# Cross attention of a fused decoder kernel: block transposes on VectorE and DMAs in place of TensorE's transposes of x

## The chip, the cores and the metric

The kernel runs on one core of one Trainium2 chip. The metric is the device time of one execution in microseconds (us). The time before is the median of three runs.

The engines are written as the profile writes them: PE is TensorE (PEld its weight loads), DVE is VectorE, ACT is ScalarE, POOL is GpSimd and SP is SyncE. SP computes nothing here; it issues DMAs, one instruction after another.

## What is computed

Two decoder layers, each with a self-mixing block, a cross attention and a feed-forward block, every block followed by a sum with its input and a layer norm. The change touches the cross attention of the first layer and the linear block behind it. `x` is 4 x 1024 x 512 (32 tiles of 128 tokens by 512), the context `ctx` has 64 rows for each of the 4 batches, and there are 16 heads of 32:

```python
q = x @ Wq.T + bq                       # for every token
s = (q_h . k_h) / sqrt(32), masked      # 16 heads x 64 keys for every token
p = softmax(s)
x = layernorm(x + (p_h . v_h joined) @ Wo.T + bo)
x = layernorm(x + tanh(x @ W12 + bias)) # the linear block, its weights folded into one matrix
```

All of it is float32. TensorE contracts over the partitions, so for `x @ W` it needs x with features on the partitions, whereas x lies in SBUF with tokens on them. x has to be turned twice in this stage: before the queries, and after the first layer norm before the linear block.

## The kernel before

The stage is `cross_attention_and_linears`. x stays in SBUF as 32 tiles; `x_tile(n)` is one. Each engine runs a list of steps written out by hand, in **slots** `s`: in slot s a tile n = s gets its scores, while tile s-2 is at its output projection, tile s-3 at its linear and so on. The order of an engine's steps inside a slot is the order of the `if there(...)` lines; nothing is scheduled by a compiler. Steps of different engines meet by semaphores, and an engine whose next instruction waits does nothing else.

TensorE's slot s, in order: `transpose_x(s+8)` turns a tile of x by four 128x128 transposes into PSUM (L954), from which ScalarE copies it to `XT` (L1052); `transpose_p(s-2)` turns the softmax weights (L994); `query(s+4)` computes a quarter of the features of the queries of a whole **group** of four tiles (L977), so four slots make one group's queries and the first of them needs all four turned tiles; `weigh(s-2)` (L1002); `transpose_x2(s-3)`, four more transposes (L954, too) for the linear; `scores(s)` (L986); `project(s-2)` (L1012); `linear(s-3)` (L1022).

VectorE's slot s: `biased(s-4)` (L1131), `total(s-1)` (L1102, L1105), `added(s-4)` (L1136 and the statistics L1109, L1111, L1114), `masked(s)` (L1090), the second layer norm's `normal` (L1119), `shifted(s)` (the maximum L1096 and its subtraction L1098, which wait for GpSimd's `hide`, L921), `attended(s-2)` (L1125 and statistics), and the first layer norm's `normal` (L1119 again, which waits for a power that GpSimd takes, L948).

SP issues six loads at the start of the stage and then nothing; `XT` has two halves, `XT[g % 2]` for group g. TensorE's PSUM banks 5 and 6 go round between query, project and linear.

Some moves of the same kind as the new ones exist elsewhere in this kernel: in the last stage VectorE transposes x in 32x32 blocks into `X4B` (L2282) and SP moves the 16 blocks to their places by 16 DMAs (L2025, `tl_XT<-tl_X4B`); in the local attention SP stores block-transposed tiles to DRAM by four DMAs each (L1286, `unit_gT<-tiles`).

## Time and profile before

| what | value |
|---|---|
| median of 3 runs | 2664.42 us (2663.8 to 2665.64) |
| the profiled execution, its own time | 2665.74 us |
| its span in the trace | 2664.0 us |
| the stage in the span | from 394.6 us to 906.1 us |
| TensorE busy over the span | 95% |
| VectorE busy over the span | 73% |

The profiled execution was 1.3 us above the median. The stage's start is TensorE's first transpose at 394.61 us and its end the last layer norm on VectorE (905.50 us and 0.55 us). The page's chain that ended last begins at 1559 us, in the last stage, so it says nothing on this one; the stage has to be read from the timeline of its engines.

### The profile page before, as it was taken

The page shows a single profiled execution, that of the slowest core. Times are in us where ns is not written, and L with a number is a line of the kernel's source. Part 1 is how long each engine was busy: PE and PEld are TensorE (multiplying, and loading weights), DVE is VectorE, ACT ScalarE, POOL GpSimd, SP SyncE. Part 2 cuts the span into 40 slices and gives each one's busy share as a digit, 9 for nine tenths or more (in the row PEclk, how much of TensorE's full clock was granted, in tenths as well). Part 3 has the DMA queues.
Part 4 walks back from the last instruction along what each step waited for, and adds up shares of the span by engine and source line. Part 5 has one row for each costly group of instructions (what it writes and reads, how often), then busy time and mean ns, then how long its engine had stood idle before and what let it go on. Part 6 is the DMA issues. An engine that isn't in the chain of part 4 may idle for free. (4 is left out here: it accounts for less than half of the span.)

```text
span 2664.0 us, 37090 instructions
## 1 busy us (share of the span) xinstructions
PE 2535.6 (95%) x12933; PEld 1562.9 (59%) x12933; DVE 1933.4 (73%) x3292; ACT 732.0 (27%) x1073; POOL 867.0 (33%) x900
## 2 busy tenths in 40 slices
PE   8999998999999898999998869999999999999998
PEld 4444544555555444445444447777777777777775
DVE  4788403666667446777778858888888888888886
ACT  1111222333332125666668711000000000000000
POOL 2322203455555336767677721111111111111000
PEclk9999999999999999999999989999999999999999
DMA  5444121000000043343434441222222222222111
GB/s 177 146 143 178 56 91 42 1 0 1 1 1 1 23 103 96 101 106 97 104 102 129 134 122 42 53 53 53 53 54 54 54 54 54 54 54 54 46 38 38
DMA packets 338726, 183.85 MB, mean 69 GB/s; under 512 B 174031, under 2 KB 304463, under 8 KB 337518
## 3 DMA queue, kind: packets, MB, share of 16 engines
q1 hardware_dynamic: 307862, 156.49, 21.4%
q10 hardware_dynamic: 30680, 24.98, 3.3%
q8 instruction: 106, 1.74, 0.3%
q14 instruction: 78, 0.64, 0.1%
HBM read 90.51 MB, written 52.43 MB: 54 GB/s over the span
## 5 line engine op out<-in xcount | busy, mean ns | idle before, releaser
L2114 PE MATMUL bank<-tiles,tl_XQT 128*128 128x512 f32 (+1 forms) x768 | 323.9, 565 | 1.2 <-issue 1.2
L2119 PE MATMUL bank<-tiles,tl_XQT 128*128 128x512 f32 (+1 forms) x768 | 317.9, 557 | 0.0
L2131 PE MATMUL bank<-tiles,tl_HT 128*128 128x512 f32 x682 | 302.1, 599 | 5.8 <-DMA tl_HT<-tl_tmp 5.8
L2114 PEld LDWEIGHTS bank<-tiles,tl_XQT 128*128 128x128 f32 x768 | 235.6, 309 | 79.8 <-issue 16.0
L2119 PEld LDWEIGHTS bank<-tiles,tl_XQT 128*128 128x128 f32 x768 | 236.7, 308 | 65.6
L2193 ACT ACTIVATE tl_HQ<-bank 128x512 f32<-128x512 f32 (+1 forms) x96 | 54.0, 562 | 803.1 <-PE bank L2114 757.0
L2131 PEld LDWEIGHTS bank<-tiles,tl_HT 128*128 128x128 f32 x682 | 219.3, 324 | 74.4 <-issue 9.4
L1403 POOL TENSOR_SCALAR_AFFINE_SELECT tiles<-tiles 128x512 f32<-128x512 f32 x256 | 184.0, 721 | 169.2 <-ACT tiles L1630 153.8
L2061 POOL TENSOR_TENSOR tl_rs<-tl_ve,mhalf 128x1 f32<-128x1 f32 x29 | 16.0, 551 | 527.5 <-DVE tl_ve L2272 527.5
L1730 DVE SCALAR_TENSOR_TENSOR tiles<-tiles,bank 128x1024 f32<-128x1024 f32 (+1 forms) x128 | 141.7, 1148 | 18.8 <-PE bank L1506 18.7
L1408 POOL TENSOR_SCALAR_AFFINE_SELECT tiles<-tiles 128x512 f32<-128x512 f32 x224 | 152.9, 682 | 0.0
L2053 POOL TENSOR_TENSOR tl_rs<-tl_ve,mhalf 128x1 f32<-128x1 f32 x32 | 18.8, 587 | 393.9 <-DVE tl_ve L2254 393.9
L1630 ACT ACTIVATE tiles<-bank 128x1024 f32<-128x1024 f32 (+1 forms) x128 | 123.5, 965 | 28.1 <-PE bank L1465 28.0
L1635 ACT ACTIVATE tiles<-tiles 128x1024 f32<-128x1024 f32 (+1 forms) x128 | 124.9, 1000 | 20.2 <-DVE tiles L1730 17.2
L1555 PE MATMUL bank<-home_T,tiles 128*128 128x512 f32 x256 | 121.2, 618 | 3.6 <-ACT tiles L1664 0.9
L977 PE MATMUL bank<-space_T 128*128 128x512 f32 x256 | 118.4, 606 | 2.5 <-DVE X L1125 2.3
L1567 PE MATMUL bank<-home_odd,tiles 128*128 128x512 f32 x256 | 117.4, 601 | 0.0
L1022 PE MATMUL bank<-space_T,space_quant 128*128 128x512 f32 x256 | 115.2, 592 | 1.5 <-ACT space_quant L1079 1.5
L1012 PE MATMUL bank<-space_even,space_quant 128*128 128x512 f32 x256 | 115.3, 593 | 1.0 <-ACT space_quant L1074 0.9
L1428 POOL TENSOR_TENSOR la_rn<-la_n,mhalf 128x16 f32<-128x16 f32 x32 | 92.8, 2899 | 52.0 <-DVE la_n L1805 52.0
L2069 PE MATMUL bank<-home_T,attended_values 128*128 128x512 f32 x232 | 106.6, 603 | 0.0
L921 POOL TENSOR_TENSOR xl_SM<-xl_SM,xl_nm 128x1024 f32<-128x1024 f32 x32 | 80.0, 2500 | 78.4 <-DVE xl_SM L1090 78.4
(302 smaller groups left out, 4669.3 us busy)
## 6 DMA issues: line engine op xcount, KB each, us to landing
tl_HT<-tl_tmp SPq DMA_DIRECT2D x248, 44.0 KB, 2.0
tl_HT<-tl_tmp ACTq DMA_DIRECT2D x248, 44.0 KB, 2.0
fp_weights<-space_quant ACTq DMA_DIRECT2D x33, 256.0 KB, 2.1
X<-in_x SPq DMA_DIRECT2D x8, 1024.0 KB, 10.2
v<-tiles SPq DMA_DIRECT2D x32, 256.0 KB, 2.4
unit_g<-tiles SPq DMA_DIRECT2D x32, 256.0 KB, 2.5
unit_gT<-tiles SPq DMA_DIRECT2D x128, 64.0 KB, 2.1
la_GN<-unit_g SPq DMA_DIRECT2D x128, 64.0 KB, 2.1
```

Source lines behind the costliest of these rows:

```text
L977: mm = e.matmul(bank[turn(s, 0)][:, :], WqT[:, c, m * P:(m + 1) * P], XT[g % 2][:, c, :], start=(c == 0), stop=(c == C - 1))
L1012: mm = e.matmul(bank[turn(s, 1)][:, :], AT[:, c, :], WoT[:, c, :], start=(c == 0), stop=(c == C - 1))
L1403: return e.affine_select(out=x[:, :, 0:P], in_=x[:, :, 0:P], compare_op=ALU.is_ge, fill=fill, base=0, pattern=[[0, HC], [1, P]], channel_m ...
L1408: return e.affine_select(out=x[:, :, P:WIN], in_=x[:, :, P:WIN], compare_op=ALU.is_ge, fill=fill, base=0, pattern=[[0, HC], [-1, P]], chan ...
L1555: mm = e.matmul(bank[1][:, :], XT[m % 2][:, c, :], WgT[:, c, :], start=(c == 0), stop=(c == C - 1))
L1567: mm = e.matmul(bank[2][:, :], XT[m % 2][:, c, :], WvT[:, c, :], start=(c == 0), stop=(c == C - 1))
L1630: e.activation(TR[p % RING][:, :, 0:cols(t)], four(ARG[:, :])[:, :, 0:cols(t)], ACT.Tanh).then_inc(s_T.sem, 1)
L1635: e.activation(y, y, ACT.Exp).then_inc(s_p.sem, 1)
L1730: e.scalar_tensor_tensor(out=y, in0=y, scalar=1.0, in1=d, op0=ALU.add, op1=ALU.mult).then_inc(s_u.sem, 1)
L2114: mm = e.matmul(bank[(2 * q) % 3][:, 0:w], chunk(XQT[n % 2], c), WgT[q][:, :, c, :], start=(c == 0), stop=(c == C - 1))
L2119: mm = e.matmul(bank[(2 * q + 1) % 3][:, 0:w], chunk(XQT[n % 2], c), WuT[q][:, :, c, :], start=(c == 0), stop=(c == C - 1))
L2131: mm = e.matmul(bank[DOWN][:, :], chunk(HT, q), WdT[:, q, :], start=(q == 0), stop=(q == IC - 1))
```

## The change

The first eight tiles are still turned by TensorE. For tiles 8 to 31, VectorE transposes the tile in 32x32 blocks into `XB` (`x_turned`) and SP moves the blocks to `XT` by 16 DMAs (`x_moved`), each of 32 partitions x 4 x 32 elements. For the linears of tiles 0 to 29, VectorE transposes the tile into `XB2` (`x2_turned`), SP stores it to a DRAM buffer by 4 DMAs of 32 x 4 x 128 elements (`x2_stored`), and ScalarE issues one load of it into `XL`; tiles 30 and 31 still go by TensorE. The linear moves from the end of slot n+3 to slot n+4, right behind the query. On VectorE `added` and its layer norm move one slot later too, and `biased` moves behind `added`. The stage has one slot more. The weights' layout of the linear is unchanged; `XL` is read with a stride of four elements.

```diff
...
+        self.X2d = self.dram("x2_turned", (2, P, D))
...
+        XB = [sb(f"XB{n}", [P, D]) for n in range(2)]
+        s_xt, d_xt = sem("x_turned"), [sem(f"xT_moved{n}") for n in range(2)]
...
+        BY_PE = 2 * B
         x_bank = lambda n: n if n < B else XTB
+        later = lambda n: BY_PE <= n < NT
...
-        SLOTS = range(-2 * B, NT + 5)
+        SLOTS = range(-2 * B, NT + 6)
+
+
+        by_blocks = lambda n: 0 <= n < NT - 2
+        XB2 = [sb(f"XB2{n}", [P, D]) for n in range(2)]
+        XLT = XL[:, :, :].rearrange("p c t -> p (c t)")
+        in_chunks = lambda x: x.rearrange("p (t c) -> p c t", c=C)
+        s_tu, d_tu, d_xl = sem("x2_turned"), [sem(f"x2_stored{n}") for n in range(2)], sem("x2T_load")
...
+                def x_moved(n):
+                    g, at = n // B, n % B * P
+                    e.wait_ge(s_xt.sem, s_xt.at(n - BY_PE + 1))
+                    e.wait_ge(s_q.sem, s_q.at(C * (g - 1)))
+                    for i in range(4):
+                        for j in range(4):
+                            e.dma_start(XT[g % 2][32 * j:32 * j + 32, :, at + 32 * i:at + 32 * i + 32],
+                                        XB[n % 2][32 * i:32 * i + 32, :].rearrange("p (c j t) -> p j c t", c=C, j=4)[:, j]
+                                        ).then_inc(d_xt[n % 2].sem, 16)
+
+                def x2_stored(n):
+
+                    e.wait_ge(s_tu.sem, s_tu.at(n + 1))
+                    e.wait_ge(d_xl.sem, d_xl.at(16 * (n - 1)))
+                    for i in range(4):
+                        e.dma_start(k.X2d[n % 2].rearrange("(j p) w -> p j w", j=4)[:, :, P * i:P * i + P],
+                                    XB2[n % 2][32 * i:32 * i + 32, :].rearrange("p (j w) -> p j w", j=4)).then_inc(d_tu[n % 2].sem, 16)
...
+                for s in SLOTS:
+                    if by_blocks(s - 3):
+                        x2_stored(s - 3)
+                    if later(s + 2 * B):
+                        x_moved(s + 2 * B)
...
                 def transpose_x2(n):
                     e.wait_ge(s_x2.sem, s_x2.at(n + 1))
-                    e.wait_ge(s_tc.sem, s_tc.at(min(n + 12, NT)))
-                    e.wait_ge(s_xe.sem, s_xe.at(n))
+                    e.wait_ge(s_tc.sem, s_tc.at(BY_PE))
+                    e.wait_ge(s_xe.sem, s_xe.at(n - NT + 2))
                     transposed(XTB, x_tile(n), s_xl)
...
                 def query(i):
 
                     g, m = i // C, i % C
-                    e.wait_ge(s_tc.sem, s_tc.at(B * g + B))
+                    e.wait_ge(s_tc.sem, s_tc.at(min(B * g + B, BY_PE)))
+                    for d in d_xt:
+                        e.wait_ge(d.sem, d.at(256 * (B // 2) * (g - 1)))
                     s = i - B
                     e.wait_ge(s_qe.sem, s_qe.at(i - 1))
-                    e.wait_ge(s_a2.sem, s_a2.at(s - 2))
+
+                    e.wait_ge(s_lbd.sem, s_lbd.at(s - 4))
...
+                    e.wait_ge(s_qe.sem, s_qe.at(min(s + B + 1, NT)))
+                    e.wait_ge(s_lbd.sem, s_lbd.at(n - 2))
+                    for c in range(C):
+                        mm = e.matmul(bank[turn(s, 2)][:, :], AT[:, c, :], WoT[:, c, :], start=(c == 0), stop=(c == C - 1))
+                    mm.then_inc(s_o.sem, 1)
+
+                def linear(n):
+                    s = n + 4
+                    if by_blocks(n):
+                        e.wait_ge(d_xl.sem, d_xl.at(16 * (n + 1)))
+                    else:
+                        e.wait_ge(s_xe.sem, s_xe.at(n - NT + 3))
+
+                    e.wait_ge(s_a2.sem, s_a2.at(min(s - 2, NT)))
                     e.wait_ge(s_lbd.sem, s_lbd.at(n - 1))
                     for c in range(C):
-                        mm = e.matmul(bank[turn(s, 1)][:, :], AT[:, c, :], WoT[:, c, :], start=(c == 0), stop=(c == C - 1))
-                    mm.then_inc(s_o.sem, 1)
-
-                def linear(n):
-                    s = n + 3
-                    e.wait_ge(s_xe.sem, s_xe.at(n + 1))
-
-                    e.wait_ge(s_qe.sem, s_qe.at(min(s + B + 1, NT)))
-                    e.wait_ge(s_a2.sem, s_a2.at(min(n, NT)))
-                    for c in range(C):
-                        mm = e.matmul(bank[turn(s, 2)][:, :], XL[:, c, :], WF[:, c, :], start=(c == 0), stop=(c == C - 1))
+                        mm = e.matmul(bank[turn(s, 1)][:, :], in_chunks(XLT)[:, c, :], WF[:, c, :], start=(c == 0), stop=(c == C - 1))
                     mm.then_inc(s_l.sem, 1)
...
-                    if there(s + 2 * B):
+                    if 0 <= s + 2 * B < BY_PE:
                         transpose_x(s + 2 * B)
                     if there(s - 2):
                         transpose_p(s - 2)
                     if there(s + B):
                         query(s + B)
+                    if there(s - 4):
+                        linear(s - 4)
                     if there(s - 2):
                         weigh(s - 2)
-                    if there(s - 3):
+                    if there(s - 3) and not by_blocks(s - 3):
                         transpose_x2(s - 3)
                     if there(s):
                         scores(s)
                     if there(s - 2):
                         project(s - 2)
-                    if there(s - 3):
-                        linear(s - 3)
...
-                    if there(s - 3):
+                    if by_blocks(s - 3):
                         n = s - 3
-                        e.wait_ge(s_xl.sem, s_xl.at(n + 1))
+                        e.wait_ge(d_tu[n % 2].sem, d_tu[n % 2].at(64 * (n // 2 + 1)))
                         e.wait_ge(s_l.sem, s_l.at(n))
-                        e.activation(XL[:, :, :], four(bank[XTB][:, :]), ACT.Copy).then_inc(s_xe.sem, 1)
+                        e.dma_start(XLT, k.X2d[n % 2]).then_inc(d_xl.sem, 16)
+                    elif there(s - 3):
+                        n = s - 3
+                        e.wait_ge(s_xl.sem, s_xl.at(n - NT + 3))
+                        e.wait_ge(s_l.sem, s_l.at(n))
+                        e.activation(in_chunks(XLT), four(bank[XTB][:, :]), ACT.Copy).then_inc(s_xe.sem, 1)
+                    if there(s - 4):
+                        n = s - 4
+                        e.wait_ge(s_lbd.sem, s_lbd.at(n + 1))
+                        e.activation(TH[:, :], TH[:, :], ACT.Tanh).then_inc(s_th.sem, 1)
...
+                def x_turned(n):
+                    e.wait_ge(d_xt[n % 2].sem, d_xt[n % 2].at(256 * ((n - BY_PE) // 2)))
+                    e.transpose(XB[n % 2][:, :], x_tile(n)).then_inc(s_xt.sem, 1)
+
+                def x2_turned(n):
+                    e.wait_ge(s_x2.sem, s_x2.at(n + 1))
+                    e.wait_ge(d_tu[n % 2].sem, d_tu[n % 2].at(64 * (n // 2)))
+                    e.transpose(XB2[n % 2][:, :].rearrange("p (j r c) -> p c j r", j=4, r=32), x_tile(n)).then_inc(s_tu.sem, 1)
...
                 for s in SLOTS:
+                    if there(s - 1):
+                        total(s - 1)
+                    if there(s - 5):
+                        added(s - 5)
                     if there(s - 4):
                         biased(s - 4)
-                    if there(s - 1):
-                        total(s - 1)
-                    if there(s - 4):
-                        added(s - 4)
                     if there(s):
                         masked(s)
-                    if there(s - 4):
-                        normal(s - 4, mv3, rs3, s_r3, s_x3)
+                    if there(s - 5):
+                        normal(s - 5, mv3, rs3, s_r3, s_x3)
+                    if later(s + 2 * B + 1):
+                        x_turned(s + 2 * B + 1)
                     if there(s):
                         shifted(s)
                     if there(s - 2):
                         attended(s - 2)
                         normal(s - 2, mv2, rs2, s_r2, s_x2)
+                    if by_blocks(s - 2):
+                        x2_turned(s - 2)
...```

On PE, one early slot of the kernel before (slot 6). `ident` with `X` is a transpose of x, `xl_SM` are the softmax weights, `space_T` alone is a query:

```order
L954 MATMUL bank<-ident,X 128x128 x4
L994 MATMUL bank<-ident,xl_SM 128x128 x8
L977 MATMUL bank<-space_T 128x512 x4
L1002 MATMUL bank<-xl_PT,space_quant 64x128 x8
L954 MATMUL bank<-ident,X 128x128 x4
L986 MATMUL bank<-space_quant,space_T 128x256 x4
L1012 MATMUL bank<-space_even,space_quant 128x512 x4
L1022 MATMUL bank<-space_T,space_quant 128x512 x4
```

And the same slot of the changed kernel (L1018 is the query, L1067 the linear, L1054 the projection):

```order
L1035 MATMUL bank<-ident,xl_SM 128x128 x8
L1018 MATMUL bank<-space_T 128x512 x4
L1067 MATMUL bank<-space_T,space_quant 128x512 x4
L1043 MATMUL bank<-xl_PT,space_quant 64x128 x8
L1027 MATMUL bank<-space_quant,space_T 128x256 x4
L1054 MATMUL bank<-space_even,space_quant 128x512 x4
```

Both groups of transposes of X are gone, the linear stands ahead of `weigh` and the scores, and the query waits for the DMAs of both halves of `XB` (the loop over `d_xt` in the diff).

On SP, the stage's first slots of the changed kernel; the kernel before has no row here. `space_T` is `XT`, and `x_turned` is the DRAM buffer of the linears.

```order
L938 DMA home_bias<-in_L_attn_bg 128x512
L921 DMA space_T<-xl_XB 32x4x32 x48
L930 DMA x_turned<-xl_XB 32x4x128 x4
L921 DMA space_T<-xl_XB 32x4x32 x16
L930 DMA x_turned<-xl_XB 32x4x128 x4
L921 DMA space_T<-xl_XB 32x4x32 x16
```

These are the moves of tiles 8, 9 and 10 (48 DMAs), the store of tile 0, the move of tile 11, the store of tile 1 and the move of tile 12. From there on each slot has one store for the linears and then one move for the queries, in this order.

On DVE, of one slot of the changed kernel, from `masked` on:

```order
L1139 TENSOR_TENSOR xl_SM<-bank,xl_mf 128x1024
L1168 TENSOR_SCALAR X<-X,xl_mv,xl_rs 128x512
L1190 STREAM_TRANSPOSE xl_XB<-X 128x512
L1145 TENSOR_REDUCE xl_mx<-xl_SM 128x16
L1147 TENSOR_TENSOR xl_SM<-xl_SM,xl_mx 128x1024
L1174 TENSOR_TENSOR X<-bank,X 128x512
L1158 BN_STATS xl_st<-X 128x6
L1160 BN_AGGR xl_mv<-xl_st 128x2
L1163 TENSOR_SCALAR xl_ve<-xl_mv 128x1
L1168 TENSOR_SCALAR X<-X,xl_mv,xl_rs 128x512
L1195 STREAM_TRANSPOSE xl_XB<-X 128x4x128
L1151 TENSOR_REDUCE xl_sm<-xl_SM 128x16
```

The kernel before has the same rows without the two STREAM_TRANSPOSE, and with the bias of the linear ahead of the last row here.

## Rows read from the trace of the kernel before

**Rows 1.** Page: engine totals (busy us, share, instructions).
```profile
span 2664.0 us, 37090 instructions
PE 2535.6 (95%) x12933; PEld 1562.9 (59%) x12933; DVE 1933.4 (73%) x3292; ACT 732.0 (27%) x1073; POOL 867.0 (33%) x900
```

**Rows 2.** Timeline, PE, one slot: start, us, engine, line, operation, count.
```profile
717.59 0.60 PE L954 MATMUL bank<-ident,X 128*128 128x128 f32 x4
718.02 1.04 PE L994 MATMUL bank<-ident,xl_SM 128*128 128x128 f32 x8
718.90 3.60 PE L977 MATMUL bank<-space_T 128*128 128x512 f32 x8
722.42 1.09 PE L1002 MATMUL bank<-xl_PT,space_quant 128*64 128x128 f32 x16
723.45 0.66 PE L954 MATMUL bank<-ident,X 128*128 128x128 f32 x4
723.94 1.89 PE L986 MATMUL bank<-space_quant,space_T 128*128 128x256 f32 x8
725.67 3.60 PE L1012 MATMUL bank<-space_even,space_quant 128*128 128x512 f32 x8
729.11 3.60 PE L1022 MATMUL bank<-space_T,space_quant 128*128 128x512 f32 x8
```

**Rows 3.** Timeline, DVE, slot 22; in brackets the idle before and its releaser.
```profile
740.83 1.23 DVE L1090 TENSOR_TENSOR xl_SM<-bank,xl_mf 128x1024 f32<-128x1024 f32 x1 [1.92 <-PE bank L986]
741.97 0.54 DVE L1119 TENSOR_SCALAR X<-X,xl_mv,xl_rs 128x512 f32<-128x512 f32 x1
744.74 1.22 DVE L1096 TENSOR_REDUCE xl_mx<-xl_SM 128x16 f32<-128x1024 f32 x1 [2.23 <-POOL xl_SM L921]
749.62 0.55 DVE L1119 TENSOR_SCALAR X<-X,xl_mv,xl_rs 128x512 f32<-128x512 f32 x1 [0.67 <-POOL xl_rs L948]
...
755.78 1.22 DVE L1090 TENSOR_TENSOR xl_SM<-bank,xl_mf 128x1024 f32<-128x1024 f32 x1 [1.92 <-PE bank L986]
```

**Rows 4.** Timeline, DVE: `masked` of slots 24, 28, 29 and 31.
```profile
770.29 1.23 DVE L1090 TENSOR_TENSOR xl_SM<-bank,xl_mf 128x1024 f32<-128x1024 f32 x1 [1.48 <-PE bank L986]
...
826.83 1.22 DVE L1090 TENSOR_TENSOR xl_SM<-bank,xl_mf 128x1024 f32<-128x1024 f32 x1
839.89 1.23 DVE L1090 TENSOR_TENSOR xl_SM<-bank,xl_mf 128x1024 f32<-128x1024 f32 x1
...
866.55 1.23 DVE L1090 TENSOR_TENSOR xl_SM<-bank,xl_mf 128x1024 f32<-128x1024 f32 x1 [0.48 <-PE bank L986]
```

**Rows 5.** One line's instructions, DVE: count, ns min/median/max, first and last start.
```profile
L2282 DVE STREAM_TRANSPOSE tl_X4B<-X x30: 703/705/711, 1569.0 to 2515.1; 128x512 f32<-128x512 f32 x30
L2400 DVE STREAM_TRANSPOSE tl_QB<-tl_XQ x31: 1082/1116/1144, 1594.9 to 2602.8; 128x512 f32<-128x512 f32 x31
```

**Rows 6.** Timeline, SP: a store by 4 DMAs, a move by 16; then landing.
```profile
1010.85 1.95 SPq L1286 DMA_DIRECT2D unit_gT<-tiles  x4
2014.39 10.33 SPq L2025 DMA_DIRECT2D tl_XT<-tl_X4B  x16
L2025 SPq DMA_DIRECT2D tl_XT<-tl_X4B x480: 591/601/1442, 1569.7 to 2525.5; - x160
DMA to landing us min/median/max: 1.8/1.8/3.0
```

**Rows 7.** Timeline, DVE: the first layer norm of tile 0.
```profile
449.64 0.55 DVE L1119 TENSOR_SCALAR X<-X,xl_mv,xl_rs 128x512 f32<-128x512 f32 x1 [0.69 <-POOL xl_rs L948]
```

**Rows 8.** Timeline, PE, after waits; the first is `query(7)`, the others as cut there.
```profile
447.96 5.37 PE L977 MATMUL bank<-space_T 128*128 128x512 f32 x8 [2.27 <-DVE X L1125]
...
464.69 0.59 PE L977 MATMUL bank<-space_T 128*128 128x512 f32 x1
...
763.32 1.88 PE L977 MATMUL bank<-space_T 128*128 128x512 f32 x4
```

**Rows 9.** Windows: PE, PEld, DVE, ACT, POOL busy, then PEclk, DMA share, GB/s.
```profile
446.00:448.00 2.00, 0.04 (x1) 0.07 (x1) 1.97 (x3) 0.75 (x1) 0.00 (x0) 1.00 0.00 0
448.00:451.50 3.50, 3.50 (x5) 1.44 (x6) 2.71 (x6) 1.71 (x3) 0.57 (x1) 0.62 0.01 2
860.00:864.00 4.00, 2.52 (x21) 2.19 (x22) 3.23 (x7) 2.42 (x4) 0.55 (x1) 0.73 0.00 0
```

**Rows 10.** Timeline, PE and DVE: the start of the next stage, the end of this.
```profile
905.50 0.55 DVE L1119 TENSOR_SCALAR X<-X,xl_mv,xl_rs 128x512 f32<-128x512 f32 x1 [0.67 <-POOL xl_rs L939]
908.97 5.69 PE L1555 MATMUL bank<-home_T,tiles 128*128 128x512 f32 x8 [0.94 <-ACT tiles L1664]
```

More of the change, by code:

```diff
@@ L930, in add_bias @@
                         e.wait_ge(s_lb.sem, s_lb.at(32))
-                    e.wait_ge(s_t.sem, s_t.at(n + 1))
+                    e.wait_ge(s_t.sem, s_t.at(min(n + 1, BY_PE)))
+                    e.wait_ge(s_xt.sem, s_xt.at(n - BY_PE + 1))
                     e.tensor_tensor(x_tile(n), x_tile(n), bo[:, :], ALU.add).then_inc(s_xb.sem, 1)
@@ L936, in _ @@
                         weights(s - 1)
-                    if there(s - 4):
-                        e.wait_ge(s_v3.sem, s_v3.at(s - 3))
+                    if there(s - 5):
+                        e.wait_ge(s_v3.sem, s_v3.at(s - 4))
                         e.tensor_tensor(rs3[:, :], ve3[:, :], k.mhalf[:, 0:1], ALU.pow).then_inc(s_r3.sem, 1)
@@ L957, in transpose_x @@
                 def transpose_x(n):
-                    e.wait_ge(s_xe.sem, s_xe.at(n - 11))
                     if n > B:
@@ L1047, in _ @@
                 for s in SLOTS:
-                    if there(s + 2 * B):
+                    if 0 <= s + 2 * B < BY_PE:
                         n = s + 2 * B
                         e.wait_ge(s_t.sem, s_t.at(n + 1))
-                        e.wait_ge(s_q.sem, s_q.at(C * (n // B - 1)))
-                        e.activation(XT[(n // B) % 2][:, :, (n % B) * P:(n % B + 1) * P], four(bank[x_bank(n)][:, :]), ACT.Copy).then_inc(s_tc.sem, 1)
+                        e.activation(XT[n // B][:, :, (n % B) * P:(n % B + 1) * P], four(bank[x_bank(n)][:, :]), ACT.Copy).then_inc(s_tc.sem, 1)
                     if there(s - 2):
@@ L1057, in _ @@
                         e.activation(PT[:, :, :], PTB.rearrange("p (n t) -> p n t", n=H // 2), ACT.Copy).then_inc(s_pe.sem, 1)
-                    if there(s - 4):
-                        n = s - 4
-                        e.wait_ge(s_lbd.sem, s_lbd.at(n + 1))
-                        e.activation(TH[:, :], TH[:, :], ACT.Tanh).then_inc(s_th.sem, 1)
                     if there(s + B):
@@ L1124, in attended @@
                     e.wait_ge(s_xb.sem, s_xb.at(n + 1))
-                    e.tensor_tensor(y, bank[turn(n + 2, 1)][:, :], y, ALU.add).then_inc(s_a2.sem, 1)
+                    e.tensor_tensor(y, bank[turn(n + 2, 2)][:, :], y, ALU.add).then_inc(s_a2.sem, 1)
                     statistics(n, y, st2, mv2, ve2, s_a2, s_t2, s_m2, s_v2, s_r2)
@@ L1130, in biased @@
                     e.wait_ge(s_a3.sem, s_a3.at(n))
-                    e.tensor_tensor(TH[:, :], bank[turn(n + 3, 2)][:, :], lb[:, :], ALU.add).then_inc(s_lbd.sem, 1)
+                    e.tensor_tensor(TH[:, :], bank[turn(n + 4, 1)][:, :], lb[:, :], ALU.add).then_inc(s_lbd.sem, 1)
                 def added(n):
@@ L1142, in _ @@
                 for s in SLOTS:
+                    if there(s - 1):
+                        total(s - 1)
+                    if there(s - 5):
+                        added(s - 5)
                     if there(s - 4):
                         biased(s - 4)
-                    if there(s - 1):
-                        total(s - 1)
-                    if there(s - 4):
-                        added(s - 4)
                     if there(s):
                         masked(s)
-                    if there(s - 4):
-                        normal(s - 4, mv3, rs3, s_r3, s_x3)
+                    if there(s - 5):
+                        normal(s - 5, mv3, rs3, s_r3, s_x3)
+                    if later(s + 2 * B + 1):
+                        x_turned(s + 2 * B + 1)
                     if there(s):
```

## The prediction, made before the changed kernel ran

> **What bounds the kernel now.** I read the page's totals first: TensorE is busy 95% of the span [rows 1]. The page's chain lies in the last stage, which is not touched, so I went to TensorE's timeline inside this stage. A slot there begins 14.95 us after the last one and has no idle time between its groups; the two groups of four transposes take 718.02 - 717.59 = 0.43 us and 723.94 - 723.45 = 0.49 us of it, the query 3.52, `weigh` 1.03, the scores 1.73, projection and linear 3.44 each and the transpose of the weights 0.88 [rows 2]. VectorE is next: from one `masked` to the end of its slot it works or waits for its own chain for 13.0 us, and then idles 1.92 us for TensorE's scores [rows 3]. In slots 28 and 29, where TensorE has no query left, `masked` no longer waits and the spacing is 839.89 - 826.83 = 13.06 us [rows 4]. That is VectorE's own round. SP is idle in the stage.
>
> **TensorE's part.** From slot 0 the slot loses 0.43 and 0.49 us and becomes 14.02 us. If nothing else came, 24 tiles for queries and 30 for linears would give 24 x 0.43 + 30 x 0.49 = 25 us. ScalarE loses the two copies behind them and has room.
>
> **VectorE's part.** `x_turned` has the form of L2282: 0.71 us. It stands behind the first `normal` (which ends at 742.51), where VectorE waits until 744.74 for GpSimd [rows 3], so it costs nothing; without that wait it would cost 0.7 us a slot. `x2_turned` writes with a stride of four as L2400 does: 1.12 us rather than 0.71 [rows 5]; I take 1.12, since the output's stride is the same. It stands behind the second `normal`, with no wait ahead of it that it could fill. VectorE's round becomes 13.06 + 1.12 = 14.18 us, just above TensorE's 14.02. So VectorE sets the slot, and by this alone it gains 14.95 - 14.18 = 0.77 us.
>
> **SP's part, on which I rest the forecast.** In every slot SP issues 4 DMAs for the linears, then 16 for the queries. The nearest rows, of the same shapes, give 1.95 us for four stores and 10.33 us for sixteen moves, 0.646 us apart, and 1.8 us until one lands [rows 6]. 12.3 us fits into a slot. But look at when it starts. The query that opens group g (slot 4g-4) needs tile 4g+3. Its move stands on SP in slot 4g-5 behind the store of tile 4g-8, and this store waits for `x2_turned(4g-8)`, which is VectorE's work of slot 4g-6, done only when TensorE is already in slot 4g-5. The loop from one such query to the next, four slots on, is then a chain:
> - query 3.52, linear 3.44, `weigh` 1.03, scores until their end 1.89: 9.9 us, with `masked` behind it [rows 2];
> - from `masked` to the end of the second `normal`, 749.62 + 0.55 - 740.83 = 9.34 us [rows 3], and `x2_turned` 1.12: 10.5 us. This turns tile 4g-6, seen from the query of group g;
> - two rounds of VectorE to `x2_turned(4g-4)`: 28.4 us;
> - on SP, the store 1.95, fifteen spacings 9.69, the last landing 1.8: 13.4 us, and the query of group g+1 may start.
>
> The sum is 62.2 us. Four slots without a wait would be 56.7 us by VectorE and 56.1 by TensorE; TensorE thus stands still for about 6 us before each group's first query. Before, four slots take 59.8 us. The change takes away a cost of 0.9 us a slot and puts a wait of 6 us in every fourth one.
>
> **The clock behind the wait.** After an idle time of 2.27 us the query at 447.96 takes 5.37 us instead of 3.60, 1.8 us more [rows 8], and the granted clock there is 0.62, in part the lower level of 1.2 GHz, after 1.00 [rows 9]. After over 5 us idle, the first matmuls of the next stage need 5.69 us for what takes 3.60 at full clock, 2.1 us more [rows 10]. I take 2.1 us for each wait; it falls into the first link of the chain (query, linear), so it counts in full. The ends are 0 (the clock is kept) and 2.7 (half clock for 5.4 us). The loop becomes 62.2 + 2.1 = 64.3 us, 4.5 more than before.
>
> **The sum**, against the profiled execution's 2665.74 us:
> - Up to query(8): the layer norm of tile 0 ends at 450.19 us [rows 7]; 1.12 + 13.4 us of transposition and SP bring the query to 464.8 us; before it is at 464.69 [rows 8]. 0 us. The wait is there too, in place of the transposes.
> - From query(8) to query(28), five loops: 5 x 4.5 = +22.5 us.
> - Query(28) to its slot's `masked`: before 770.29 - 763.32 = 7.0 us [rows 4, 8]; now 9.9, since the linear stands between, and 2.1 of clock: +5.0 us.
> - `masked` of slot 24 to slot 31: before 866.55 - 770.29 = 96.3 us [rows 4]; now 7 x 14.18 = 99.3: +3.0 us. The transposes that are gone no longer help here, the one on VectorE still costs.
> - In slots 28 to 31 TensorE idles some 3.7 us of each slot, and the clock falls as it does at 860 us, 0.73 [rows 9], where two slots took 866.55 - 839.89 = 26.7 us instead of 26.1 [rows 4]: +1 us, ends 0 and 7 (half clock on the whole path from scores on in four slots).
> - From there to the end of the stage, 906.05 - 866.55 = 39.5 us [rows 4, 10], the linears of tiles 30 and 31 wait for nothing new: 0 us, at most +2.
>
> Together +31.5 us: 2697.2 us for the profiled execution, and, 1.3 us lower as before, 2696 us for the median. So the change makes it 1.2% slower; a measurement of this kernel tells about 0.2% (5 us) from no change.
>
> **A rule of the Trainium skill.** Sixteen DMAs in a row held SP for 10.33 us while one took 1.8 us to land [rows 6], so here the issue is the long part. The Trainium skill says in "DMA: Bandwidth & Descriptors", section "Issuing engines are not separate DMA queues", that the sequencer's time to start a DMA is usually small relative to the DMA itself. By that rule rival 1 would hold; the trace speaks against it. The page "VectorE: DVE Perf Modes", section "Rules for kernel authors", advises TensorE for a transpose of 128x128 where PSUM will do, which speaks against this change without a price.
>
> **Rivals.**
> 1. *The moves come in time, and it gets faster.* If SP needs so little that the last landing is no later than the unstalled query, 6 us sooner (13.4 down to 7.4 us, 0.27 us per move), VectorE's round alone sets 20 slots: query(8) to query(28) takes 283.6 us instead of 298.6, and the query's way to `masked` +2.9, the tail +3.0. With some 4 us of wait left out at the start that is -13 us: 2651 us. It turns at a gain of 4.5 us a loop, a spacing near 0.35 us with the clock's cost, 0.50 without. The smallest of 480 such issues was 0.591 us [rows 6], so 10%.
> 2. *The clock is kept*: no 2.1 us in six waits, none in the tail: 2696 - 13.6 = 2682 us. Against it stand [rows 8 to 10]; 10%.
> 3. *The landing takes longer*: 3.0 us is the longest seen [rows 6], and the tail's clock costs its 7 us: 6 x 1.2 + 6 = +13, 2709 us. Sixteen moves, a store and ScalarE's load share the DMA engines in each slot, as comparable ones do in the last stage. 12%.
> 4. *The change does nothing*: the loop takes as long as before, 59.8 us, because part of the wait goes and the clock stays: 2659 to 2670 us; 5%.
> 5. My forecast's own case, 58%; 5% is left for something slower still, above 2716 us.
>
> **How the numbers follow.** 2696 us is the likeliest case. Its own unknowns: spacing 0.59 to 0.65 (-0.8 us a wait), the clock's cost 0 to 2.7 us, the landing, the tail. Taking in rivals 2 and 3 the range is 2674 to 2716 us and leaves out rivals 1 and 4 and the far end, two in ten. Faster by over 0.2%: 0.11 (rival 1 and a little of 4), within 0.2%: 0.05, slower: 0.84.
>
> **What the profile after would show.** On TensorE's timeline, waits of 5 to 7 us before queries 8, 12, 16, 20, 24 and 28, released by the DMA `space_T<-xl_XB`, and a granted clock near 0.5 right behind them; the other three slots of a group near 14.1 us. On SP, 16 moves in 10.3 us, starting when 4 stores of 1.95 us are done, and these starting at `x2_turned`. On VectorE, transposes of 0.71 and 1.12 us, and a spacing of 14.2 us between the `masked` of the last slots. I am wrong if the spacing of the moves is far below 0.6 us, if the query's wait is missing, or if another wait, such as ScalarE's load of `XL` before the linear (it should have some 5 us to spare), comes in its place.

## The result, and the profile after

| what | before | changed |
|---|---|---|
| median of four runs each | 2665.03 us (2663.8 to 2668.03) | 2702.34 us (2698.55 to 2702.8) |
| ratio, 95% interval | | 1.0137 (1.0125 to 1.015) |
| profiled execution, own time | 2665.74 us | 2702.51 us |
| its span | 2664.0 us | 2700.8 us |
| end of the stage in the span | 906.05 us | 942.29 us |

The change makes the kernel 37 us slower, 1.4%. The stage ends 36.2 us later and the rest of the program takes 0.6 us more, so the loss is in the stage. A note for all comparisons below: in the profiled executions of all kernels the unchanged code behind the stage took 1755.0 to 1760.8 us, so differences of a few us are read from the stage's own length and not from the medians.

The page of the changed kernel, its totals and the groups of query and linear (busy us, mean ns | idle us before them):

```profile
PE 2532.9 (94%) x12717; PEld 1577.7 (58%) x12717; DVE 1978.5 (73%) x3346; ACT 698.5 (26%) x1019; POOL 865.3 (32%) x900
L1018 PE MATMUL bank<-space_T 128*128 128x512 f32 x256 | 130.5, 659 | 37.0 <-issue 37.0
L1067 PE MATMUL bank<-space_T,space_quant 128*128 128x512 f32 x256 | 120.1, 614 | 16.5 <-issue 15.3
```

Against [rows 1] TensorE has 216 matmuls fewer and is busy only 2.7 us less. The query's line says why: its 32 queries take 130.5 us, 4.08 us each, though a query at full clock takes 3.60, and TensorE sat idle for 37.0 us ahead of them. TensorE's timeline shows where; this is one slot without and one with the wait (start, duration, in brackets the idle time before it):

```profile
504.04 3.60 PE L1054 MATMUL bank<-space_even,space_quant 128*128 128x512 f32 x8
507.47 1.04 PE L1035 MATMUL bank<-ident,xl_SM 128*128 128x128 f32 x8
508.35 3.60 PE L1018 MATMUL bank<-space_T 128*128 128x512 f32 x8
...
521.60 1.04 PE L1035 MATMUL bank<-ident,xl_SM 128*128 128x128 f32 x8
528.30 5.83 PE L1018 MATMUL bank<-space_T 128*128 128x512 f32 x8 [5.67 <-issue]
533.97 3.60 PE L1067 MATMUL bank<-space_T,space_quant 128*128 128x512 f32 x8
537.49 1.10 PE L1043 MATMUL bank<-xl_PT,space_quant 128*64 128x128 f32 x16
538.52 1.99 PE L1027 MATMUL bank<-space_quant,space_T 128*128 128x256 f32 x8
```

A slot without the wait now takes 521.60 - 507.47 = 14.13 us, against 14.95 before [rows 2]. The query at 528.30 opens a group; it starts after 5.67 us of nothing and takes 2.2 us longer. The same query of the other groups:

```profile
464.04 5.53 PE L1018 MATMUL bank<-space_T 128*128 128x512 f32 x8 [8.38 <-issue]
...
592.88 5.96 PE L1018 MATMUL bank<-space_T 128*128 128x512 f32 x8 [5.68 <-issue]
657.57 6.05 PE L1018 MATMUL bank<-space_T 128*128 128x512 f32 x8 [5.67 <-issue]
722.37 6.07 PE L1018 MATMUL bank<-space_T 128*128 128x512 f32 x8 [5.70 <-issue]
787.36 6.00 PE L1018 MATMUL bank<-space_T 128*128 128x512 f32 x8 [5.86 <-issue]
```

These are queries 8, 16, 20, 24 and 28. 8.38 + 5.67 + 5.68 + 5.67 + 5.70 + 5.86 is the 37.0 us of the page. "issue" says that the profile has no record that ended the wait; what the query waits for in the code are the sixteen moves of the group's last tile, and their rows on SP end 1.4 us before it (from issue to landing one takes 1.8 us in the median):

```profile
514.76 1.76 SPq L930 DMA_DIRECT2D x_turned<-xl_XB  x4
516.62 10.25 SPq L921 DMA_DIRECT2D space_T<-xl_XB  x16
528.86 1.76 SPq L930 DMA_DIRECT2D x_turned<-xl_XB  x4
530.72 10.26 SPq L921 DMA_DIRECT2D space_T<-xl_XB  x16
551.07 1.76 SPq L930 DMA_DIRECT2D x_turned<-xl_XB  x4
```

516.62 + 10.25 = 526.87 is the end of the last issue of tile 15, the last of the group that query 12, at 528.30, opens. SP does nothing between 541.0 and 551.07: it is not full, it is late, because the store waits for VectorE. VectorE's rows around the wait:

```profile
527.75 1.09 DVE L1195 STREAM_TRANSPOSE xl_XB<-X 128x512 f32<-128x512 f32 x1
...
537.60 0.69 DVE L1180 TENSOR_TENSOR xl_TH<-bank,xl_lb 128x512 f32<-128x512 f32 x1 [5.79 <-PE bank L1067]
540.55 1.23 DVE L1139 TENSOR_TENSOR xl_SM<-bank,xl_mf 128x1024 f32<-128x1024 f32 x1 [2.26 <-PE bank L1027]
...
549.94 1.11 DVE L1195 STREAM_TRANSPOSE xl_XB<-X 128x512 f32<-128x512 f32 x1
```

`x2_turned` ends at 528.84 and 551.05, and SP's stores start at 528.86 and 551.07. VectorE itself stands still for 5.79 and 2.26 us, for TensorE. So this is the loop of the prediction: query, `masked`, `x2_turned`, store, moves, next group's query. Cut at these rows, from 528.30 to the query at 592.88: 12.25 us to `masked` (540.55), 10.50 to the end of `x2_turned` (551.05), 28.25 for two slots (549.94 to 578.19 by `masked` at 540.55 and 568.80), and 13.58 for SP and the landing; 64.58 us.

The granted clock around the wait (window, PE, PEld, DVE, ACT, POOL busy, then PEclk, DMA share, GB/s):

```profile
522.30:528.30 6.00, 0.33 (x4) 0.12 (x2) 5.17 (x8) 1.97 (x2) 1.73 (x2) 0.79 0.16 26
528.30:533.00 4.70, 4.70 (x6) 2.02 (x7) 3.37 (x7) 0.00 (x0) 2.72 (x2) 0.54 0.25 63
533.00:544.00 11.00, 11.00 (x45) 6.83 (x44) 2.99 (x4) 1.80 (x3) 2.08 (x1) 1.00 0.23 46
```

It falls within the idle time, stands near 0.5, the level of 1.2 GHz, for the query, and is back at 1.00, 2.4 GHz, with the linear. In the last slots TensorE has a new wait, ahead of the linear, sometimes with the lower clock behind it and sometimes not:

```profile
849.26 5.49 PE L1067 MATMUL bank<-space_T,space_quant 128*128 128x512 f32 x8 [2.84 <-issue]
...
864.84 3.79 PE L1067 MATMUL bank<-space_T,space_quant 128*128 128x512 f32 x8 [2.83 <-issue]
...
878.83 3.79 PE L1067 MATMUL bank<-space_T,space_quant 128*128 128x512 f32 x8 [2.94 <-issue]
...
906.80 5.49 PE L1067 MATMUL bank<-space_T,space_quant 128*128 128x512 f32 x8 [2.94 <-issue]
```

These are slots 28, 29, 30 and 32. The linear's row of the page, 16.5 us of idle time, is mostly this wait.

### The profile page after: what moved, and what is told of

Read it like the earlier page. It is cut to its first block and busy times, and to the rows that moved or that the text cites. A ratio compares the mean times of both kernels' runs of the same rounds, so it can differ in the third digit from the quotient of the medians.

```text
span 2700.8 us, 37250 instructions
## 1 busy us (share of the span) xinstructions
PE 2532.9 (94%) x12717; PEld 1577.7 (58%) x12717; DVE 1978.5 (73%) x3346; ACT 698.5 (26%) x1019; POOL 865.3 (32%) x900
## 5 line engine op out<-in xcount | busy, mean ns | idle before, releaser
L1018 PE MATMUL bank<-space_T 128*128 128x512 f32 x256 | 130.5, 659 | 37.0 <-issue 37.0
L1067 PE MATMUL bank<-space_T,space_quant 128*128 128x512 f32 x256 | 120.1, 614 | 16.5 <-issue 15.3
L1054 PE MATMUL bank<-space_even,space_quant 128*128 128x512 f32 x256 | 115.3, 593 | 0.8 <-ACT space_quant L1114 0.7
L1067 PEld LDWEIGHTS bank<-space_T,space_quant 128*128 128x128 f32 x256 | 78.6, 310 | 53.4 <-issue 27.1
```

The source lines that it names most:

```text
L1018: mm = e.matmul(bank[turn(s, 0)][:, :], WqT[:, c, m * P:(m + 1) * P], XT[g % 2][:, c, :], start=(c == 0), stop=(c == C - 1))
L1067: mm = e.matmul(bank[turn(s, 1)][:, :], in_chunks(XLT)[:, c, :], WF[:, c, :], start=(c == 0), stop=(c == C - 1))
```

## Experiments

My theory: the loop through SP's queue costs a wait in each group, because (a) each move stands behind a store that waits for VectorE, (b) sixteen issues take 10.3 us, and (c) the wait lowers the clock. Rivals: the wait is the landing's or the DMA engines'; the linears' way through DRAM costs the time; the clock plays no part. Each diff is against the changed kernel. Medians, ratios to the kernel before with their 95% intervals, and the stage from `masked(0)` to its last layer norm's end in the profiled execution. The kernel before was measured again beside them, 2665.79 us beside the first four variants (to "queries alone") and 2666.1 us beside the other four:

| kernel | median us | ratio to before | stage, us |
|---|---|---|---|
| before | 2665.79, 2666.1 | | 486.3 |
| changed | 2702.34 | 1.0137 (1.0125 to 1.015) | 523.0 |
| moves first | 2655.53 | 0.9964 (0.9952 to 0.9977) | 480.4 |
| TensorE kept busy | 2691.75 | 1.01 (1.0086 to 1.0115) | 512.9 |
| half the moves | 2663.72 | 0.9995 (0.9986 to 1.0004) | 484.2 |
| queries alone | 2663.84 | 0.9995 (0.9987 to 1.0004) | 484.3 |
| linears alone | 2666.09 | 0.9999 (0.999 to 1.0008) | 484.9 |
| moves first, busy last slots | 2656.93 | 0.9969 (0.9957 to 0.998) | 478.7 |
| moves first, own banks | 2649.0 | 0.9935 (0.9923 to 0.9948) | 470.2 |
| the same, linears by blocks to tile 24 | 2643.87 | 0.9923 (0.9909 to 0.9936) | 464.7 |

### The moves ahead of the store

```diff
                 for s in SLOTS:
-                    if by_blocks(s - 3):
-                        x2_stored(s - 3)
                     if later(s + 2 * B):
                         x_moved(s + 2 * B)
+                    if by_blocks(s - 3):
+                        x2_stored(s - 3)
```

> Only the order on SP is changed: in each slot the 16 moves of a tile for the queries stand ahead of the 4 stores of a tile for the linears. Theory (the move waits, through the store ahead of it, for VectorE's work on another tile): a move starts as soon as its own tile is turned, some 9 us sooner, the wait before each group's first query (5.7 us) and the half clock behind it go, and each slot takes TensorE's 14.12 us. Query(28) then comes 282.4 us after query(8) instead of 323.3, query(8) itself some 6 us sooner, and of the part behind query(28) 2.9 + 3.6 + 3.1 us over before remain: about 2652 us, 0.5% faster than before. Rival A (there is too much issue time on SP, whatever the order: 12.1 us and the landings): the wait stays at several us, only the victim changes, and the linears wait for XL; 2680 us or more. Rival B (VectorE's two transposes set the slot): no wait at the queries, but slots above 14.2 us and waits for VectorE; 2660 us or more.

SP does the same work in another order, and 2702 us become 2655.5: faster than the kernel before, though not the 2652 us expected (the last slots, below). No query waits but the first of group 2. SP's rows at the place of the wait above (the same view):

```profile
514.76 10.25 SPq L921 DMA_DIRECT2D space_T<-xl_XB  x16
525.11 1.99 SPq L930 DMA_DIRECT2D x_turned<-xl_XB  x4
528.88 11.00 SPq L921 DMA_DIRECT2D space_T<-xl_XB  x16
```

A run of sixteen still takes 10.25 us. It starts every 14.12 us and ends well before its query, so the length of the run alone did not make the wait: its place behind the store did. The slots take 14.12 us throughout. But the last four are long:

```profile
740.00:795.00 55.00, 55.00 (x222) 33.87 (x221) 41.99 (x68) 15.20 (x21) 29.89 (x22) 1.00 0.14 39
795.00:811.00 16.00, 13.16 (x51) 7.59 (x50) 11.65 (x18) 3.72 (x5) 7.39 (x6) 0.89 0.18 50
811.00:826.00 15.00, 12.17 (x48) 6.95 (x47) 10.28 (x18) 3.08 (x4) 7.02 (x5) 0.89 0.11 36
```

Each of slots 28 to 31 has 2.84 us of idle time, then a linear of 5.1 to 5.5 us (these are TensorE's rows), and `masked` comes every 15.4 us on the mean, 61.54 us for four (794.92 to 856.46):

```profile
802.02 5.11 PE L1067 MATMUL bank<-space_T,space_quant 128*128 128x512 f32 x8 [2.84 <-issue]
817.22 5.49 PE L1067 MATMUL bank<-space_T,space_quant 128*128 128x512 f32 x8 [2.83 <-issue]
```

### TensorE kept busy through the wait

Six matmuls that nobody reads stand ahead of the first query of groups 2 to 7.

```diff
                     e.wait_ge(s_tc.sem, s_tc.at(min(B * g + B, BY_PE)))
+                    if g >= 2 and m == 0:
+                        for _ in range(6):
+                            e.matmul(bank[XTB][:, :], WqT[:, 0, 0:P], WF[:, 0, :], start=True, stop=True)
                     for d in d_xt:
```

> The changed kernel with six matmuls (128x512, into an unused bank, result not read) ahead of the first query of each group from the third on, in the place of the wait: 6 x 0.858 = 5.1 us of TensorE's work where it stands idle for 5.7 to 8.4 us. Theory (the clock falls in the wait and costs 2.3 us behind it): the query takes 3.6 us instead of 5.5 to 6.1, the loop of four slots falls from 64.7 to about 62.4 us, and six of these give 12 to 14 us: about 2689 us. Rival (the query is slow because the DMAs write XT and the SBUF is busy, or the clock doesn't matter because the chain goes another way): the loop stays at 64.7 us and the time at 2702 us.

2691.75 us, 10.6 less than the changed kernel, with work added. The query at the same place:

```profile
518.71 5.32 PE L1013 MATMUL bank<-space_T 128*128 128x512 f32 x12
524.43 3.67 PE L1021 MATMUL bank<-space_T 128*128 128x512 f32 x8 [0.41 <-issue]
```

It still comes when the moves have landed, but at full speed. The loop is 62.3 us (524.43 to 586.73) in place of 64.6, so the clock costs 2.3 us a loop; the other 2.5 us over the 59.8 of before are the chain. Six times 2.3 would be 13.8, and 13.9 us are won up to `masked` of slot 24; 4.2 of them are lost again in the last four slots, which are all long here (61.8 us, 826.10 to 887.86, against 57.6, 842.16 to 899.71).

### Half of the moves

Only eight of the sixteen DMAs of each tile are issued, so for tokens 64 to 127 of the later tiles the queries read what was there before.

```diff
-                    for i in range(4):
+                    for i in range(2):
                         for j in range(4):
...
-                        e.wait_ge(d.sem, d.at(256 * (B // 2) * (g - 1)))
+                        e.wait_ge(d.sem, d.at(128 * (B // 2) * (g - 1)))
...
```

> Of the 16 DMAs that move a tile for the queries only 8 are issued (token rows 0 to 63; the other half of XT keeps old values, so the queries of these tokens are wrong). SP's order is that of the changed kernel. Theory (the loop is a chain with SP's issue time in it): SP's link is 8 x 0.646 = 5.2 us shorter, the wait falls from 5.7 to about 0.5 us, the clock is kept, and the loop is TensorE's 4 x 14.12 = 56.5 us plus 0.5: five loops give 38 us, the first wait and clock some 7 more: about 2656 us. Rival A (a landing or the DMA engines' load sets the time, not the issue): the wait falls by less than half. Rival B (VectorE's chain alone): no change, 2702 us.

The order on SP is that of the changed kernel, and the wait shrinks from 5.7 to 0.5 us (TensorE's queries 12 and 16):

```profile
515.80 3.67 PE L1018 MATMUL bank<-space_T 128*128 128x512 f32 x8 [0.52 <-issue]
...
573.06 3.67 PE L1018 MATMUL bank<-space_T 128*128 128x512 f32 x8 [0.53 <-issue]
```

The loop is 57.26 us: the 64.3 us of the prediction less eight spacings of 0.64 and less 2.1 of clock give 57.1. So the count of issues, 0.6 us each, is the other half of the cause; the landing is no shorter here (median 1.9 us against 1.8 in the changed kernel). The time, 2663.7 us, missed the expected 2656. The five loops gave 34.5 us in place of 38 (745.71 - 456.85 = 288.86 us against 323.32). And from `masked` of slot 24 to that of slot 31 this kernel needs 102.65 us (755.80 to 858.45) against 99.93, since here, too, three of the last four slots take 15.2 to 15.6 us. I had not put that into the expectation.

### Each half of the change alone

Without blocks for the linears (`by_blocks` is never true), SP has only the moves:

```diff
-        by_blocks = lambda n: 0 <= n < NT - 2
+        N2 = 0
+        by_blocks = lambda n: 0 <= n < N2
...
```

> Only the queries' x goes by blocks; the linears' x is turned by TensorE and copied by ScalarE for all 32 tiles, at its new place in the order. No x2_turned on VectorE, no stores on SP. Theory: nothing stands ahead of the moves on SP, no wait; TensorE's slot is 14.12 + 0.4 = 14.5 us up to slot 31 where it sets the pace, VectorE's round 13.06; 20 slots x (14.95 - 14.5) = 9 us gained, some 5 lost by the linear that stands between query and scores and by the slot more: about 2660 us, 0.2% faster than before. Rival (the moves alone, 10.3 us on SP with landing, already come late): waits of some us at the groups' first queries, 2675 us or more.

And without blocks for the queries, SP has only the stores:

```diff
-        BY_PE = 2 * B
+        BY_PE = NT
...
-                    for d in d_xt:
-                        e.wait_ge(d.sem, d.at(256 * (B // 2) * (g - 1)))
...
```

> Only the linears' half of the change: x for the queries is turned by TensorE for all 32 tiles, SP has only the four stores of a slot. Theory (the sixteen moves behind the store are what makes the queries wait): no idle time of over 1 us ahead of any query, every slot of TensorE near 14.12 + 0.44 = 14.57 us (VectorE's round 13.99 less 0.71 us of the first transposition stays below it), so 20 slots gain 0.38 us each, 7.6 us, and the first slots some 3; the rest of the stage costs what it did in the changed kernel, 5.5 less 2.3 (no clock loss at a query) + 3.65 + 3.1 = 10 us. Together within 3 us of the kernel before, near 2665 us. Rival (the linears' own chain, store, load and strided reading, costs by itself): idle time ahead of the linear in every slot, slots of 15 us or more, 2675 us or more.

2663.84 and 2666.09 us: neither half alone differs from before, and neither is 37 us slower. `masked` comes every 14.51 and 14.56 us with no wait at a query but 1.5 us at the first of group 2 with the queries alone, so each gains its four transposes, 0.4 us a slot. `masked(0)` already starts 2.2 us earlier with the linears alone (417.49 against 419.72), so I count from there: `masked` of slot 24 comes 11.2 and 12.0 us sooner than before. The slots behind it give most of this back: with the linears alone it is -12.0 us at slot 24, -4.2 at slot 31 and -1.4 at the stage's end. (My expectation took 0.71 us off VectorE's 13.99; that was an error, since the slots in which 13.99 was read hold no first transposition.) The two halves are harmless apart and cost 37 us together: the wait is in the queue that they share. A rival of mine, that the way through DRAM costs the linears their time, falls with this, and with the load's landing, 2.5 to 3.1 us, which no linear waited for in the middle of the stage.

### The clock in the last slots

Moves first, and three matmuls that nobody reads ahead of the linear from slot 28 on.

```diff
...
+                    if not there(s + B):
+                        for _ in range(3):
+                            e.matmul(bank[XTB][:, :], WoT[:, 0, 0:P], WF[:, 0, :], start=True, stop=True)
                     e.wait_ge(s_a2.sem, s_a2.at(min(s - 2, NT)))
```

> The moves stand ahead of the store, and from slot 28 on TensorE makes three more matmuls, whose result nobody reads, ahead of the linear, where it idled 2.84 us. Theory (in slots 28 to 31 the spacing of 15.4 us instead of 13.99 comes from the lower clock behind this idle time): the linear takes 3.6 us instead of 5.3, the granted clock is 1.00 in slots 28 to 31, masked comes every 14.0 us, four times 1.4 us = 6 us less than with the moves first alone: 2650 us. Rival (the spacing comes from what is waited for, and the slow matmuls are its effect only): spacing stays near 15.4 us with a clock of 1.00, 2655 us; the added matmuls may not lengthen it by more than 1 us.

The mechanism came out, the time did not. In the same windows as above the clock is full:

```profile
795.00:811.00 16.00, 15.79 (x60) 9.12 (x59) 12.31 (x19) 3.67 (x5) 8.12 (x7) 1.00 0.18 50
811.00:826.00 15.00, 14.67 (x58) 8.56 (x57) 10.77 (x17) 3.19 (x4) 8.04 (x6) 1.00 0.13 36
```

With less idle time left, the profile also names what the linear waits for; L1177 is `attended`:

```profile
815.90 3.82 PE L1070 MATMUL bank<-space_T,space_quant 128*128 128x512 f32 x8 [0.33 <-DVE X L1177]
```

Four slots take 55.97 us (794.86 to 850.83) in place of 61.54, so 5.6 of the expected 6 us came. But from there to the stage's end it is 46.95 us where it was 43.86, as the added matmuls also stand in the four slots after the last scores, where nothing hides them. The stage gains 1.7 us, and the median, 2656.93 us, can't be told from 2655.53.

### The cause of the wait in the last slots

Moves first; from slot 28 on, where no query needs them, PSUM bank 5 belongs to the linear and bank 6 to the projection. The linear then waits for the bias of the linear before it and no longer for `attended`; the projection, at the end of the slot, waits for `attended` in its place.

```diff
+        linear_bank = lambda s: turn(s, 1) if s < NT - B else 5
+        project_bank = lambda s: turn(s, 2) if s < NT - B else 6
...
+                    e.wait_ge(s_a2.sem, s_a2.at(n if s >= NT - B else 0))
...
-                    e.wait_ge(s_a2.sem, s_a2.at(min(s - 2, NT)))
-                    e.wait_ge(s_lbd.sem, s_lbd.at(n - 1))
+                    e.wait_ge(s_a2.sem, s_a2.at(min(s - 2, NT) if s < NT - B else 0))
+                    e.wait_ge(s_lbd.sem, s_lbd.at(n - 1 if s < NT - B else n))
...
```

> The moves stand ahead of the store, and in the slots from 28 on the linear has PSUM bank 5 and the projection bank 6 to themselves, so the linear waits for the bias of the linear before it and no longer for VectorE's sum of the projection two slots back. Theory (the loop through this bank sets the spacing of the last slots, with TensorE idle 2.84 us ahead of the linear): that idle time is gone from before the linear, masked of slots 28 to 31 comes every 13.0 to 14.0 us by VectorE's own round, 6 us less than with the moves first alone, 2646 to 2650 us. Rival (the idle time only moves to the place where the next wait is, ahead of the weights' transposes or the scores, and the clock falls there): spacing between 14.5 and 15.4 us, 2653 to 2656 us.

2649.0 us, 6.5 less than with the moves first; in the profiled executions the stage is 10.2 us shorter, 5.6 in the four slots and 4.6 behind them. The idle time moves, as the rival said, to `weigh` (2.4 us at most), but the slots stay at VectorE's 13.99 us (794.86 to 850.82 for four), as the theory said:

```profile
811.16 3.82 PE L1070 MATMUL bank<-space_T,space_quant 128*128 128x512 f32 x8 [0.51 <-DMA space_quant<-x_turned]
817.30 1.09 PE L1045 MATMUL bank<-xl_PT,space_quant 128*64 128x128 f32 x16 [2.32 <-ACT xl_PT L1104]
818.33 3.45 PE L1029 MATMUL bank<-space_quant,space_T 128*128 128x256 f32 x8
```

The scores at the lower clock (3.45 us in place of 1.99) cost nothing here, since VectorE is not yet waiting for them. The stage's end comes 39.26 us after the last `masked`, against 43.86 with the banks shared and 39.5 before. So the four slots return to 56.0 us either by the full clock with the banks shared, as in the experiment above, or by own banks with the lower clock still there in some slots; the bank's wait cost them time only together with the lower clock, as slots 29 to 31 of the changed kernel show as well (2.8 to 2.9 us of wait, full clock, 14.0 us a slot). The shorter end came with own banks alone.

### And VectorE without its second transposition there

The same, and the linears of tiles 25 to 31 get their x from TensorE again.

```diff
-        by_blocks = lambda n: 0 <= n < NT - 2
+        N2 = 25
+        by_blocks = lambda n: 0 <= n < N2
...
```

> As the kernel with the moves first and own banks in the last slots, and the linears of tiles 25 to 29, too, get their x from TensorE's transposes, so that VectorE is without its transposition of 1.1 us in those slots. Theory (VectorE's round sets the last slots once the bank is free): masked of slots 28 to 31 comes every 13.1 us, as in the kernel before, TensorE idles some 0.5 us in a slot more evenly, 2642 to 2648 us, the fastest of all. Rival (TensorE's idle time and its lower clock set them whatever VectorE does): spacing of 14.3 us or more, 2652 us or more.

2643.87 us, the lowest median, 0.77% below the kernel before. Its interval overlaps that of the kernel with own banks, so the medians alone do not tell the two apart; the slots do. `masked` in slots 28 and 29:

```profile
809.09 1.21 DVE L1143 TENSOR_TENSOR xl_SM<-bank,xl_mf 128x1024 f32<-128x1024 f32 x1
822.05 1.21 DVE L1143 TENSOR_TENSOR xl_SM<-bank,xl_mf 128x1024 f32<-128x1024 f32 x1
```

And the window of slot 28 to 29 (columns as above):

```profile
813.00:826.00 13.00, 11.31 (x53) 7.50 (x52) 9.81 (x17) 4.28 (x5) 7.07 (x6) 1.00 0.01 3
```

The spacing is 12.96 us and the clock 1.00, though TensorE idles 1.7 us in each of slots 29 to 31. The nearest kernel without own banks is the one with the queries alone, where TensorE turns all of the linears' x: its last slots take 14.28 us at full clock and 16.0 with the lower one (802.73, 817.01, 832.98), above VectorE's 13.06 in both cases, so there VectorE's lighter round did not set them. No run changes the banks alone with this lighter round.

## Why the prediction was right, and where its sizes were off

| step | predicted us | measured us |
|---|---|---|
| up to query(8) | 0 | -0.7 (464.04 against 464.69) |
| five loops to query(28) | +22.5 | +24.7 (323.32 against 298.63) |
| query(28) to `masked` of slot 24 | +5.0 | +5.5 (12.42 against 6.97) |
| `masked` of slot 24 to slot 31, with the clock | +4.0 | +3.7 (99.93 against 96.26) |
| from there to the stage's end | 0 | +3.1 (42.58 against 39.5) |
| sum | +31.5 | +36.2 |

The sign, the place and the mechanism were right, and the time lies in the range; 2702 us is 6 above the 2696. By its own steps:

- **The chain.** Predicted were 9.9 + 10.5 + 28.4 + 13.4 = 62.2 us; with TensorE kept busy the loop took 62.3. The sum from the rows of another stage [rows 6] held: sixteen moves 10.25 us for 10.33, landing 1.8 for 1.8, four stores 1.76 for 1.95.
- **The clock behind the wait** was mis-sized by a little. 2.1 us was taken from [rows 10]; the queries took 5.53 to 6.07 us instead of 3.60, 1.9 to 2.5 us more, and the kernel with TensorE busy gives 2.3 us a loop.
- **Which engine sets the other slots.** I said VectorE, 14.18 us. It is TensorE, with 14.12: the scores, without transposes ahead of them, take 1.83 us from their start to the projection's where they took 1.73, 0.1 us more than their old rows let expect; what the linear takes more (3.53 for 3.44), the query ahead of it takes less. VectorE's own round is 13.99 us, so `x2_turned` costs it some 0.93 and not 1.12. The two errors nearly cancel.
- **The stage's end** was the largest miss. I priced it at nothing because the linears there "wait for nothing new". They do: the linear now takes its PSUM bank from the projection of the slot before, which VectorE's `attended` has to read first. At 906.80 the linear has waited 2.94 us and then takes 5.49. With own banks the end takes 39.26 us, as before, in the same order of steps.
- **The last slots' clock.** The term of +1 us with ends of 0 and 7 held, with one of four slots long in the changed kernel. In the kernel with the moves first all four were, 5.6 us more than with the clock kept full. My bound was right and the likeliest value only lucky.
- **The releaser** of the queries' wait is not named as a DMA but as "issue", so that sign, as I put it, did not show. The SP rows had to give it.

The rivals: the smallest of 384 issues was 0.585 us, so moves in time by quicker issues (rival 1) did not come; what I had not listed is that they come in time by mere order. The clock was not kept. The landing stayed at its 1.8 us:

```profile
L921 SPq DMA_DIRECT2D space_T<-xl_XB x384: 585/601/1411, 414.2 to 785.3; - x192
DMA to landing us min/median/max: 1.8/1.8/3.2
```

The Trainium skill says in "DMA: Bandwidth & Descriptors", section "Issuing engines are not separate DMA queues", that the sequencer's time to initiate a DMA is usually small relative to the DMA itself. That is a sentence on one DMA, and here one issue of 0.601 us is a third of its landing of 1.8 us; the prediction set sixteen issues against one landing. For a run of sixteen the issues are the long part: sixteen landings one after another would be 28.8 us, but query 12 starts 11.7 us after the first issue of its run (516.62 to 528.30), so the landings lie beside the issues, and the 10.25 us of issues remain.

Two things stay open. Why the same idle time of 2.83 to 2.94 us is followed by the lower clock in some slots and not in others was not settled. And the 1755.0 to 1760.8 us of the code behind the stage differ between kernels without any edit there; it was not followed further.

## What to carry to other kernels

Before a step is put on a DMA queue, write down for the queue what each entry waits for: an entry that is urgent and ready, behind one that waits for late work, turns idle room on that queue into a wait of TensorE, and exchanging the two lines was worth 47 us here. The moves here were priced by their issues (0.6 us each), not by bytes or landing: a tile's 256 KB took 10.25 us of SP in sixteen DMAs and 1.76 us in the stores' four. When an engine is relieved, follow the next thing it needs up to the end of the loop: here a shared PSUM bank and VectorE's round in the last slots had to be relieved as well, and that took the gain from 0.4% to 0.8%.

## What the runs showed of the hardware that I had not expected

- An idle time of 2.8 us in each slot was enough for the lower level of the clock in slots 28 to 31 of two kernels, moves first and TensorE kept busy (5.1 to 5.5 us for a linear of 3.79), and 2.8 to 2.9 us left the clock alone three times in a row in the changed kernel (slots 29 to 31). 1.7 us in a slot left it at 1.00 in the fastest kernel.
- Reading the stationary x with a stride of four elements makes its load longer, 309 ns in the row below against 190 in the kernel before (L1022); the matmul row beside it stays at 593 ns (592 before), so it is hidden.

```profile
L1067 PEld LDWEIGHTS bank<-space_T,space_quant x256: 307/309/338, 469.0 to 936.8; 128*128 128x128 f32 x128
L1067 PE MATMUL bank<-space_T,space_quant x256: 592/593/1062, 469.4 to 937.2; 128*128 128x512 f32 x128
```

- Where the moves run back to back with a store behind them, the stores mostly take 1.98 us for four, and 1.76 us where SP was idle before; the difference is small beside the order's effect.
